# Attention times V in four column tiles, with the inverse row sums transposed by TensorE

## What is computed

```
# L0, twice
u_left  = h @ (h @ W_left[l].T).T / temper;  u_right likewise
u       = u_left on the upper triangle and the diagonal, u_right below it (masked by adj)
e       = exp(u) * adj
h       = relu(layer_norm((e / (sum(e, 2) + 1e-10)) @ (h @ W_lin[l].T + b_lin[l]), ln_a[l], ln_b[l]))
x       = layernorm(x + h)
# L1
q, k, v = x @ Wq.T, x @ Wk.T, x @ Wv.T + bv            # 12 heads of 32
scores  = einsum('bqhd,bkhd->bhqk', q, k) * scale + 2 * adj
scores  = where(any(scores != 0), scores, -inf)
p       = nan_to_num(softmax(scores))
x       = layernorm(x + einsum('bhqk,bkhd->bqhd', p, v).reshape(...) @ Wo.T + bo)
```

## Time and profile before

| what | value |
|---|---|
| median of 3 runs | 2787.65 us (2786.99 to 2789.58) |
| the profiled execution | 2786.43 us, its span 2784.6 us |
| busy: PE, DVE, ACT, POOL | 98%, 85%, 66%, 53% of the span |
| granted TensorE clock over the span | 0.993 |
| moved by DMA | 40 GB/s over the span |

### The profile page before, as it was taken

The page is one execution under the profiler, slowest core; times in us unless marked ns, Lnnn a source line. Parts: engine busy times, 40 slices in busy tenths (PEclk is TensorE's granted clock), DMA queues, the critical chain, the costliest instruction groups (busy, mean ns, idle before and its releaser), DMA issues.

```text
span 2784.6 us, 74097 instructions
## 1 busy us (share of the span) xinstructions
PE 2733.9 (98%) x27072; PEld 1764.9 (63%) x27072; DVE 2374.0 (85%) x8170; ACT 1846.5 (66%) x4363; POOL 1472.7 (53%) x1558
## 2 busy tenths in 40 slices
PE   6999999999999999999999999999999999999996
PEld 3566666666666666666666666666666666666664
DVE  4888988888888889888889888898888898888986
ACT  4666676666676666776666766667666667666665
POOL 3555465455555555654455644556545556445553
PEclk9999999999999999999999999999999999999998
DMA  4011011010111010110111111101111101101000
...
DMA packets 55992, 116.68 MB, mean 42 GB/s; under 512 B 4944, under 2 KB 37712, under 8 KB 55632
## 3 DMA queue, kind: packets, MB, share of 16 engines
...
## 4 chain that ended last, share of the span: by engine, by line
PE 97%; DVE 1%; issue 1%; ACT 0%; DMA 0%; POOL 0%; SPq 0%; POOLq 0%; DVEq 0%; ACTq 0%
PE psum L1242 72%; PE psum L1252 11%; PE psum L1306 7%; PE psum L1401 4%; PE psum L1375 3%; DMA s<-weights 0%; DVE s L836 0%; DVE y L899 0%; DVE st L961 0%; DVE st L907 0%; DVE o L880 0%; DVE z L1013 0%; ACT w L582 0%; DVE pT_lo L801 0%; DVE z L1022 0%
## 5 line engine op out<-in xcount | busy, mean ns | idle before, releaser
L582 ACT ACTIVATE w<-s,nmax 128x128 f32<-128x128 f32 x1536 | 480.6, 393 | 2.4 <-DVE nmax L836 2.4
L1242 PE MATMUL psum<-hT_hi,w_hi 128*128 128x512 f16 x1152 | 438.8, 381 | 12.1 <-POOL hT_lo L377 11.9
L458 POOL TENSOR_TENSOR fold<-s 128x768 f32<-128x768 f32 x128 | 242.5, 1894 | 387.6 <-DVE nmax L836 285.7
L1242 PE MATMUL psum<-hT_lo,w_hi 128*128 128x512 f16 x1152 | 437.8, 380 | 0.0
L1242 PE MATMUL psum<-hT_hi,w_lo 128*128 128x512 f16 x1152 | 437.7, 380 | 0.0
L522 ACT ACTIVATE nT_hi<-psum 128x512 f16<-128x512 f32 x384 | 227.7, 594 | 298.9 <-PE psum L1242 296.8
L836 DVE CUSTOM_DVE_ANT_0 s<-psum,adj 128x128 f32<-128x128 f32 x1536 | 339.5, 285 | 6.1 <-DVE live L856 0.5
L385 POOL TENSOR_TENSOR hl_lo<-hl_raw,hl_hi 128x384 fp32r<-128x384 f32 x256 | 238.9, 954 | 102.6 <-ACT hl_hi L522 98.3
L803 DVE SCALAR_TENSOR_TENSOR nT_lo<-psum,nT_hi 128x512 f16<-128x512 f32 x384 | 257.7, 681 | 30.6 <-ACT nT_hi L522 30.6
L801 DVE TENSOR_TENSOR pT_lo<-psum,pT_hi 128x512 f16<-128x512 f32 x384 | 251.0, 683 | 26.1 <-ACT pT_hi L522 25.7
L522 ACT ACTIVATE pT_hi<-psum 128x512 f16<-128x512 f32 x384 | 214.6, 594 | 81.5 <-PE psum L1252 80.6
...
## 6 DMA issues: line engine op xcount, KB each, us to landing
...
out<-y SPq DMA_DIRECT2D x128, 192.0 KB, 1.9
...
```

The source lines that it names most:

```text
L458: nc.gpsimd.tensor_tensor(fold[:, :, 0:n], src[:, :, 0:n], src[:, :, n:2 * n], ALU.add)\
L582: last = nc.scalar.activation(w[:, m], s[b % 2][:, m], ACT.Exp, bias=nmax[b % 2][:, m:m + 1], scale=-1.0)
L1242: last = mm(dst, a, b, start=(i == 0), stop=(i == total - 1))
```

## The change

For `pv` the operands change places. `v` of a head (32 columns) is now the stationary operand and `pT` of the head (128 columns, the queries) moves. The output of a head has its 32 features on partitions, so four heads fill the 128 partitions of a bank, each matmul in a column tile of 32. The result is already transposed, and `to` on PE is gone.

The row sums can't come from a column of ones any more. ACT's exponentials write them out (`accum_out`). `rs_of` on DVE takes the reciprocal, gates it and copies it 32 times wide into `rs` (128x384); PE turns that in three transposes (`rt`), ACT copies the result out of PSUM into `o`, and DVE multiplies `pv`'s bank by it, in place. ACT rounds `o` to `oT_hi` from SBUF, and the rest `oT_lo` is formed by POOL, no longer by DVE. `v_raw` has two buffers for four graphs, with waits of their own.

In SP's queue the store of graph 2 moves to the next pass, behind its loads, beside that of graph 3. `BANK_USES` and all five orders are written anew. The cut diff (line numbers are those of neither file):

```
-        v_raw = sb("v_raw", [GROUP, FEAT])
-        v_hi, v_lo = (sb(f"v_{p}", [GROUP, HEADS, VCOL], f16) for p in ("hi", "lo"))
+        v_raw = sb("v_raw", [2, FEAT])
+        v_hi, v_lo = (sb(f"v_{p}", [GROUP, FEAT], f16) for p in ("hi", "lo"))
+        rs = [sb(f"rs{i}", [KB, TILES, HEAD]) for i in range(2)]
+        o = [sb(f"o{i}", [KB, TOK]) for i in range(2)]
...
         BANK_USES = (
-            uses(("nl0", 0), ("th", 1), ("v", 3), ("nl1", 0), ("pv", 0), ("nl1", 4), ("pv", 2)),
+            uses(("u0", 1), ("hl0", 3), ("c0", 2), ("th", 1), ("v", 2), ("pv", 0), ("pt", 5), ("nl1", 5), ("pv", 2),
+                 ("c1", 0)),
...
+            uses(("nl0", 2, 4), ("qk", 2), ("s", 1, 5), ("pt", 2), ("s", 9), ("pt", 4), ("s", 13), ("u1", 0),
+                 ("hl1", 3), ("c1", 2)),
...
# SP
-                store(p, 3)
+                for b in range(2, GROUP):
+                    store(p, b)
...
-                for b in range(3):
+                for b in range(2):
                     store(p, b)
# POOL
+            def to(run, b):
+                pool.wait_ge(to_hi.sem, p.upto(to_hi, b + 1))
+                nc.gpsimd.tensor_tensor(oT_lo[b % 2][:], o[b % 2][:], oT_hi[b % 2][:], ALU.subtract)\
+                    .then_inc(to_lo.sem, 1)
# ACT
                     last = nc.scalar.activation(w[:, m], s[b % 2][:, m], ACT.Exp, bias=nmax[b % 2][:, m:m + 1],
-                                                scale=-1.0)
+                                                scale=-1.0, accum_out=sums[b % 2][:, m:m + 1])
+            def rt(run, b):
+                act.wait_ge(rt_full.sem, p.upto(rt_full, b + 1))
...
+                copy(o[b % 2][:].rearrange("p k t -> p (k t)"), bank("rt", b)[:, 0:FEAT]).then_inc(rt_ok.sem, 1)
...
+                act.wait_ge(o_ok.sem, p.upto(o_ok, b + 1))
+                copy(oT_hi[b % 2][:], o[b % 2][:]).then_inc(to_hi.sem, 1)
# DVE
             def rs_of(run, b):
-                dve.wait_ge(pv_full.sem, p.upto(pv_full, b + 1))
-                nc.vector.reciprocal(rs[b % 2][:], src[:, :, HEAD]).then_inc(rcp_ok.sem, 1)
+                dve.wait_ge(p_ok.sem, p.upto(p_ok, (b + 1) * TILES))
+                nc.vector.reciprocal(rcp[b % 2][:], sums[b % 2][:]).then_inc(rcp_ok.sem, 1)
...
+                wide = rcp[b % 2][:].rearrange("p (j c) -> p c j", j=TILES)[:, :, :, None]
+                nc.vector.tensor_copy(rs[b % 2][:], wide.to_broadcast([128, KB, TILES, HEAD])).then_inc(rs_ok.sem, 1)
             def pv(run, b):
-                nc.vector.tensor_tensor(o[b % 2][:].rearrange("p (c j) d -> p j c d", j=TILES), src[:, :, :, 0:HEAD],
-                                        by_tile(rs[b % 2][:])[:, :, :, None].to_broadcast([128, TILES, KB, HEAD]),
-                                        ALU.mult).then_inc(o_ok.sem, 1)
-            def to(run, b):
-                    lo(p, to_hi, b, "to", oT_lo[b % 2][:], oT_hi[b % 2][:], to_lo)
+                dve.wait_ge(pv_full.sem, p.upto(pv_full, b + 1))
+                dve.wait_ge(rt_ok.sem, p.upto(rt_ok, b + 1))
+                nc.vector.tensor_tensor(o[b % 2][:].rearrange("p k t -> p (k t)"), bank("pv", b)[:, 0:FEAT],
+                                        o[b % 2][:].rearrange("p k t -> p (k t)"), ALU.mult).then_inc(o_ok.sem, 1)
# PE
-                for n in range(HEADS):
...
+                for c in range(KB):
+                    for i in range(3):
+                        a, m = ((v_hi, pT_hi), (v_lo, pT_hi), (v_hi, pT_lo))[i]
+                        for j in range(TILES):
+                            d = slice(HEAD * j, HEAD * (j + 1))
+                            last = mm(dst[d, c * TOK:(c + 1) * TOK], a[:, b, c * 128 + HEAD * j:c * 128 + HEAD * (j + 1)],
+                                      m[b % 2][:, KB * j + c], start=(i == 0), stop=(i == 2))
                 last.then_inc(pv_full.sem, 1)
-            def to(run, b):
-                turn("to", b, [of[:, k * 128:(k + 1) * 128] for k in range(KB)], to_full)
+            def rt(run, b):
+                pe.wait_ge(rs_ok.sem, p.upto(rs_ok, b + 1))
+                run.await_bank(pe, "rt", b)
+                turn("rt", b, [rs[b % 2][:, c].rearrange("p j d -> p (j d)") for c in range(KB)], rt_full)
```

More of the change, by code:

```diff
@@ L12 @@
 GT = GROUP * TOK
-VCOL = HEAD + 1
 HCOL = FEAT + 2
@@ L180, in place @@
+            uses(("hl0", 0), ("x1t", 2), ("s", 3, 7), ("pt", 1), ("s", 11), ("rt", 1), ("s", 15), ("hl1", 2),
+                 ("rt", 2)))
+        TAIL = (("rs", 3), ("rt", 3), ("pv", 3), ("po", 3), ("fin", 2), ("fin", 3), ("y2_power", 3), ("store", 2), ("store", 3))
+        L1_STAGES = ("x1t", "qk", "v", "s", "pt", "pv", "rt", "po")
         def place(stage, i):
@@ L699, in body @@
                 ctx(p, 0, 3)
+                xt(p, 0)
                 qk(p, 2)
                 qk(p, 3)
+                xt(p, 1)
+                xt(p, 2)
                 qk(p, 4)
+                fin(p, 3)
                 qk(p, 5)
@@ L1222, in body @@
                 bn(p, 1, 2)
+                po_stats(p, 2)
+                fin(p, 1)
                 bn(p, 1, 3)
-                fin(p, 1)
             def head():
```

373 lines of the change are left out of this document (187 added, 186 removed).

## The result

The changed kernel takes 2772.02 us (median of 5 runs, 2770.45 to 2773.88) against 2787.65 us (5 runs, 2785.14 to 2789.58) before: a ratio of 0.9943, 95% interval 0.9932 to 0.9954. That is 15.6 us or 0.56% less, where 25.7 us were predicted. The profiled execution took 2771.86 us, its span 2770.1 us.

What follows compares the result with a forecast made beforehand. PE's own instruction stream was taken as the bound, 31 passes of 84.90 us. Saving 31 x (1.16 - 0.3) = 26.7 us and adding 2 gave 2786.4 - 26.7 + 2 = 2761.7, predicted as 2762 us; range 2748 to 2797.

Steps and rivals of the forecast that it cites:

- PE, `pv`: PE's `pv` stage: from 0.90 to 0.61 us, saving 0.29 us four times a pass, 1.16 us a pass.
- Rival C: In `pv`, column tiles' loads go one by one at 0.025 us: `pv` 1.01 us, total 2813 us (2795 at 0.87); chance 0.13.
- The waits: New PE waits from tight places in the new order: 0 to 1 us a pass, taken as 0.3.
- `nl` 4 in the bank of `nl` 2: PE comes to this bank after 8.7 us, DVE is done at 9.1 to 9.2: PE waits 0.3 to 0.5 us.
- two others: Tight places: `pv` 2 needing `pT_lo` (DVE 6.3 us, PE 6.6); `u` of round 1 needing `nT_lo` (2.4 against 2.9).
- rival D: Late store 0 holds `y2` of graph 2, making DVE late next pass: 1.3 to 1.6 us a pass, 2794 to 2803; chance 0.07.
- PE's bare stream: PE's instructions in a pass with both layers, without waits: 84.90 - 1.16 = 83.74 us.
- PE's 9.7 us up to `pt` 1.2: PE's work from round 1's `nl` 0 to `pt` 1.2, against about 8.8 us on ACT: holds by some 0.9 us.
- SP: Loads ahead of store 2 come some 20 us earlier in the pass; none was waited for, so nothing gained.
- I take 2 us more: Outside the passes with both layers, ACT's accumulator reads on four graphs' path: at most 4.8 us, taken as 2.
- the forecast's own 2755 to 2769: Total time if passes have waits of 0.05 to 0.5 us each; chance 0.44.
- rival B: New waits of 0.6 to 1.2 us a pass from ACT's reads or DVE's copy: 2772 to 2791 us; chance 0.21.

Runs made afterwards that it cites:

- serial_tiles: The changed kernel with `pv`'s loops exchanged, so that the nine matmuls of one column tile follow each other before the next tile: 2878.73 us.
- po2_later: The changed kernel with the sum `y` of graph 2 moved on DVE behind three `bn_stats` of `z`: 2785.36 us.
- rs_first: The changed kernel with `rs_of` 0 ahead of `nl` 0 of round 1 in DVE's order: 2766.58 us.
- no_gate: The changed kernel without DVE's gate in all passes, so rows without a live entry are not zeroed: 2762.59 us.
- fin0_early: rs_first, plus ACT's last scaling of graph 0 ahead of `to` 2 and `hl` 2 of round 1, so its store is issued earlier: 2768.28 us.
- no_sums: The changed kernel without the sums of ACT's exponentials, the reciprocal taken of the row minimum instead: 2773.9 us.
- early3: rs_first, plus graph 3's sums, transposes, product and rounding taken out of the drain pass and pulled forward in the last pass: 2763.09 us.

## Why the prediction was right, and where it was not

**PE, `pv`.** Predicted 0.61 us, measured 0.61 to 0.62, and 0.056 us for a round of four. The step rested on two rows of the kernel before, `scores` for the time of a round and `u` for the independence of column tiles. Rival C, that the loads go one by one at 0.025 us each, is refuted. So is, as a serial cost, the price of 0.96 us that the prediction worked out from the Trainium skill (TensorEngine Tiling, Restrictions and Gotchas, and TensorE: Matmul & The Clock Gate, LDWEIGHTS): no cost of a load shows, with four tiles side by side or with one (0.056 us a matmul in serial_tiles). One argument for rival C was misread: it says that 33 columns need less than half of 0.025 us, but by `scores` they need 0.056 x 33 / 128 = 0.014 us, over half.

**The waits.** Predicted 0.3 us a pass; the passes average 84.04 us as forecast. The size was right and the place was not, so the agreement to 0.01 us is luck. I had named `nl` 4 in the bank of `nl` 2 and two others. The chain has no wait at `nl` 4 in a normal pass (the 45 matmuls from there to `u` take 8.38 us in one piece), though the place is as tight as I took it for: 0.47 us more work on DVE showed there in full (po2_later). The wait was `rt` 0 on DVE's widened sums, 0.24 us in every pass (rs_first, no_gate: 83.71). The longer passes add 2.4 us over 30 passes. The late store of graph 0 is in the largest of these; fin0_early speaks for it as the larger part, and the rest is open. That store is rival D's mechanism; it came true in few passes, at up to 0.7 us instead of 1.3 to 1.6 in each. 83.71 us, a normal pass without the wait, is what I had for PE's bare stream, 83.74.

**Why `rt` 0 was not on my list.** I booked `rs_of` as "reciprocal, gate and product stay". Their own durations do, but the gate's duration depends on what POOL does at that moment: its mean went from 175 to 301 ns because it had moved in time. Removing it gave back the whole wait. The Trainium skill, SBUF — State Buffer, section Who interferes with whom, says that a DVE instruction with two SBUF inputs and a GpSimd instruction that reads SBUF exclude each other, and whichever comes later waits for the other's end. The trace agrees to 0.03 us: 0.68 and 1.46 us, both ending with POOL's instruction. POOL's instruction beside the gate of graph 0 is a `v_lo`, which the kernel before has as well; all orders were written anew, and in this one the two meet.

**ACT.** Predicted 0.10 us a read, measured 0.085 in the spacing. ACT is busy 62.7 of 83.95 us, predicted 64. Its sums held nobody up (no_sums). The terms that I listed for PE's 9.7 us up to `pt` 1.2 add up to 9.1; it takes the fifth transpose stage and the exit from a tiling to come to 9.7, and nothing hung on it.

**DVE, POOL.** The widening copy was priced at 0.475 us and takes 0.553, though it has one input; POOL's `oT_lo` at 0.885 takes 0.956. Of the first, 0.08 us more than booked stand on the way to `rt` 0.

**SP.** Nothing, as predicted.

**The end.** This is the term that failed: "I take 2 us more". It was derived from ACT's reads, which cost nothing there (no_sums: 157.2 us). By my terms the stretch behind the last `u` should have grown by 2 - 0.86 = 1.1 us; it grew by 11.0. The 9.9 us between are nearly the whole miss of 10. I had priced one instruction on a path that is no longer PE's, and had not laid the new chain (sums, widening, transposes, copy, product, rounding, rest on POOL) against the old one where nothing covers it, as I did for the full pass.

What the traces show of it: the last pass with both layers gives nothing back and costs 0.7 us up to its last denominators, where I had counted it as the 31st that saves 0.86; and graph 3's sum comes 3.2 us later behind these denominators, which covers the 2.8 us of the second stage. The 5.0 and 2.8 us of the last pass stay open. Three other orders did not bring them back, which speaks for the longer chain of each graph and against the layout, but no run takes the chain apart. no_gate gained 3.4 us at the end, but this doesn't explain the loss: the kernel before has its gates too, at 0.17 us as a rule, and in its fourth stage the clock was no more than 0.72 and `po` 0 took 3.0 us, about what it takes after the change. early3 gains 3.1 us in a part that was late before the change too, so it explains nothing of the loss either.

**The time as a whole.** 2772.0 us is in the stated range and outside of the forecast's own 2755 to 2769; it is the lower edge of rival B (2772 to 2791), whose mechanism, waits of 0.6 to 1.2 us a pass, did not come. The last step of the sum was also rounded the wrong way: 2761.7 + 1.2 is 2762.9, not 2762.
